# Where the first stage's weight loads are issued, and where the last stage waits for cleared buffers, in a four-layer kernel on one core

## What is computed

```python
x = L0_attn_x                                             # (2, 2048, 256)
x = x + ln(window_attention(ln(x), w_attn, w_proj))       # 16 heads, windows of 64
x = x + ln(moe(ln(x)))                                    # 8 experts, top 2, and a shared SwiGLU
x = x + ln(gated_linear_attention(ln(x)))                 # causal, 16 heads, gate, affine norm
x = x + ln(gated_recurrence(ln(x)))                       # scan over the leading axis, tanh head
```

```python
qkv = x @ w_attn.T;  q, k, v = split(qkv)                 # heads of 16
att = softmax(q @ k.T / sqrt(16))                         # within each window of 64 tokens
y = (att @ v) @ w_proj.T
```

## Time and profile before

| | us |
|---|---|
| median of three runs | 1522.32 |
| lowest and highest | 1518.44, 1523.31 |
| the profiled execution, its own time | 1526.08 |
| its span, first to last instruction | 1524.2 |
| PE busy in the span | 1431.7 |

### The profile page before, as it was taken

The page is one execution under the profiler, slowest core; times in us unless marked ns, Lnnn a source line. Parts: engine busy times, 40 slices in busy tenths (PEclk is TensorE's granted clock), DMA queues, the critical chain, the costliest instruction groups (busy, mean ns, idle before and its releaser), DMA issues. The chain is left out here.

```text
span 1524.2 us, 36248 instructions
## 1 busy us (share of the span) xinstructions
PE 1431.7 (94%) x13257; PEld 1248.6 (82%) x13257; DVE 871.3 (57%) x1979; ACT 712.5 (47%) x1656; POOL 603.5 (40%) x1133
## 2 busy tenths in 40 slices
PE   5999999898999999999999997998999999999985
PEld 4888888687899999999999997876777777777865
DVE  3888888364333334333433331366788888888762
ACT  3666666221344444454445442334555555555542
POOL 2565555213122222212221112434657775775432
PEclk9999999899899999999999998999999999999988
DMA  5333433253011111111111112521111211121000
GB/s 197 96 120 106 123 107 100 64 158 118 28 36 49 43 43 42 44 46 42 39 42 50 42 43 73 163 70 43 40 60 44 64 56 52 43 64 33 9 15 21
DMA packets 88044, 100.10 MB, mean 66 GB/s; under 512 B 12384, under 2 KB 74720, under 8 KB 87872
## 3 DMA queue, kind: packets, MB, share of 16 engines
q1 hardware_dynamic: 77824, 75.53, 15.9%
q0 software_dynamic: 6480, 17.70, 4.1%
q10 hardware_dynamic: 3568, 4.55, 0.9%
HBM read 63.28 MB, written 34.47 MB: 64 GB/s over the span
## 5 line engine op out<-in xcount | busy, mean ns | idle before, releaser
L895 PEld LDWEIGHTS ex_hb<-ex_xT,lane_w 128*128 128x128 f32 x3124 | 362.6, 193 | 6.5 <-issue 2.8
L895 PE MATMUL ex_hb<-ex_xT,lane_w 128*128 128x128 f32 x3124 | 363.2, 276 | 2.4 <-ACT lane_w L891 2.4
L998 DVE TENSOR_TENSOR ex_gT<-ex_gT,ex_hb 128x384 f32<-128x384 f32 (+1 forms) x142 | 69.2, 488 | 334.8 <-ACT ex_gT L961 306.9
L869 POOL COPY slot_idx<-source 128x1 int32<-128x1 int32 x69 | 37.4, 543 | 413.3 <-PE ex_xb L922 413.3
L931 PE MATMUL ex_yb<-w,ex_gT 128*128 x852 | 195.7, 379 | 1.6 <-DVE ex_gT L1000 1.6
L959 ACT ACTIVATE ex_gT<-ex_hb 128x384 f32<-128x384 f32 (+1 forms) x142 | 62.0, 437 | 247.2 <-PE ex_hb L895 246.6
L931 PEld LDWEIGHTS ex_yb<-w,ex_gT 128*128 128x128 f32 x852 | 156.3, 190 | 20.1 <-issue 1.8
L891 ACT COPY lane_w<-w 128x1408 f32 x71 | 96.9, 1365 | 7.9 <-issue 1.7
L1072 POOL TENSOR_SCALAR la_ln_ve<-la_ln_mv 128x1 f32<-128x1 f32 x128 | 33.6, 262 | 155.0 <-DVE la_ln_mv L1065 150.0
L1643 POOL DMA_INDIRECT la_a<-yg,place x64 | 69.0, 1079 | 49.9 <-POOLq L55 34.7
L1402 DVE TENSOR_TENSOR la_em<-la_E,consts 128x512 f32<-128x512 f32 x128 | 79.3, 682 | 6.9 <-PE la_E L1356 6.5
(11 more groups left out here) (263 smaller groups left out, 3162.8 us busy)
## 6 DMA issues: line engine op xcount, KB each, us to landing
yg<-ex_yo SPq DMA_DIRECT2D x71, 128.0 KB
w<-in_w SPq DMA_DIRECT2D x16, 384.0 KB, 4.9
w<-in_w SPq DMA_DIRECT2D x16, 352.0 KB
w<-in_w SPq DMA_DIRECT2D x16, 320.0 KB
wa_xa<-in_x SPq DMA_DIRECT2D x32, 128.0 KB
x<-wa_xo SPq DMA_DIRECT2D x32, 128.0 KB
xn<-wa_xn SPq DMA_DIRECT2D x32, 128.0 KB, 3.6
xn1T<-wa_x1T SPq DMA_DIRECT2D x32, 128.0 KB, 3.6
```

Source lines behind the costliest of these rows:

```text
L869: e.tensor_copy(d["idx"][:], source[:, i:i + 1]).then_inc(S["idx"], 1)
L895: o = e.matmul(out, lane_w[:, i % 2, k, at:at + P], B[i % 2]["xT"][:, k, :], start=(k == 0), stop=(k == KC - 1))
L998: o = e.tensor_tensor(g, g, chunks(hb[2 * half + 1][:, 0:n], c1 - c0), ALU.mult)
```

## The change

Five things, none of which alters a number that is computed:

- The constants come in two loads. `first` is now columns 0 to 132 (`ident`, `half`, `head_of_16`; 68 KB), and `others` the remaining 887. DVE waits for `others` before the routing's choice, PE before its prefix sums.
- `wqkv` comes in three column ranges. `keys` is the middle one (256 KB), with a semaphore of its own, and `own` is the other two and `wp`. PE waits for `keys` ahead of its first key matmul and for `own` ahead of its first query matmul. ACT issues `first`, `keys`, `own`, `others`: six DMAs.
- DVE clears `vb` at once, and sets the ones at `s == 2`, behind the first tile's statistics. ACT waits for `vb_set` ahead of its first two writes to `vb`.
- `shared` and `later` are issued by SP, behind x of tile 3 and of tile 5. The pieces of `w13` go out behind x of tiles 2, 4, ... 30 and 31, so none at tile 0.
- In `attention_recurrence` the three waits for `zero` stand at the first use: ACT in step 4, PE and DVE in step 5.

```diff
-        first = Loads(nc, "l_consts", [(consts[:], A["consts"])])
+        n = sum(lay[k].shape[1] for k in ("ident", "half", "head_of_16"))
+        first = Loads(nc, "l_consts", [(consts[:, 0:n], A["consts"][:, 0:n])])
+        others = Loads(nc, "l_more", [(consts[:, n:], A["consts"][:, n:])])
...
-        own = Loads(nc, "l_wa", [(wqkv[:], kcn(A["w_attnT"])), (wp[:], kcn(A["w_projT"]))])
+        keys = Loads(nc, "l_wk", [(wqkv[:, :, C:2 * C], kcn(A["w_attnT"])[:, :, C:2 * C])])
+        own = Loads(nc, "l_wa", [(wqkv[:, :, 0:C], kcn(A["w_attnT"])[:, :, 0:C]),
+                                 (wqkv[:, :, 2 * C:3 * C], kcn(A["w_attnT"])[:, :, 2 * C:3 * C]), (wp[:], kcn(A["w_projT"]))])
...
-                    if i % 2 == 0:
-                        for dst, src in w13_piece(i // 2):
+                    if i >= 2 and i % 2 == 0 or i == NT - 1:
+                        for dst, src in w13_piece((i - 1) // 2):
                             e.dma_start(dst, src).then_inc(S["w13"], 16)
+                    if i == 3:
+                        shared.start(e)
+                    if i == 5:
+                        later.start(e)
...
         def tensor(e):
             first.wait(e)
-            own.wait(e)
...
                     e.wait_ge(S["xnT"], i + 1)
+                    if i == 0:
+                        keys.wait(e)
...
                         e.wait_ge(S["vb"], i)
+                    else:
+                        own.wait(e)
...
-            first.wait(e)
             e.memset(B[0]["vb"][:], 0.0).then_inc(S["set"], 1)
-            e.wait_ge(S["set"], 2)
-            for d in B:
-                for w in range(2):
-                    for h2 in range(2):
-                        o = e.memset(d["vb"][64 * h2:64 * h2 + 64, w, :, h2, D:D + 1], 1.0)
-            o.then_inc(S["vb_set"], 1)
             for s in range(STEPS):
+                if s == 2:
+                    first.wait(e)
+                    e.wait_ge(S["set"], 2)
...
+                    o.then_inc(S["vb_set"], 1)
...
             first.start(e)
+            keys.start(e)
             own.start(e)
-            e.wait_ge(S["vb_set"], 1)
+            others.start(e)
             for s in range(STEPS):
-                if s == 2:
-                    shared.start(e)
-                if s == 4:
-                    later.start(e)
...
                         e.wait_ge(S["pv"], i - 1)
+                    else:
+                        e.wait_ge(S["vb_set"], 1)
```

21 lines of the change are left out of this document (15 added, 6 removed).

## The result

| | before | changed |
|---|---|---|
| median (us) | 1522.12, 6 runs | 1512.18, 6 runs |
| lowest and highest | 1517.76, 1525.55 | 1508.80, 1516.29 |
| ratio, 95% interval | | 0.9938, 0.9919 to 0.9956 |
| the profiled execution, its own time | 1526.08 | 1516.29 |

The changed kernel is 9.9 us faster by the medians, and 0.62% by the ratio. Timed a second time on another occasion it took 1510.29 us (1504.37 to 1515.05, 6 runs), beside 1523.48 for the kernel before (11 runs): 13.2 us, ratio 0.9919, 0.9896 to 0.9943. Most of the distance between single runs goes with the mean granted clock: 1504.37 at 0.989, about 1510 at 0.985, 1515 to 1516 at 0.980.

What follows compares the result with a forecast made beforehand. Two chains of short steps, at the start and in the last stage, were taken to bound it; 3.6 + 3.9 + 2.6 = 10.1 us off 1526.08 gave 1516.0, as a median 1512.2, with 8 in 10 between 1507.5 and 1518.

Steps and rivals of the forecast that it cites:

- A: First tile: split loads, later ones in vb and w13 pieces; norm at 6.0, gain 3.6 us (2.5 to 4.4).
- B: Third tile: shared and later issued by SyncE; no idle time or low clock, gain 3.9 us (2.4 to 4.4).
- C: Last stage's start: moved waits for zero let TensorE's late tiles begin earlier, gain 2.6 us (1.4 to 2.9).
- the landing of x: Kernel start: first x and small constants land at 3.8 us, between 3.0 at the earliest and 4.9 at the latest.
- The table load: ScalarE at the start: six issues end at 3.7 us and the table load at 5.0, before the shift is complete.
- The weights: First tile: keys through at 4.0 us and own at 6.0, with 3.9 and 3.8 us to spare.
- near 26.6: Sign of being right, first stage: the third scores come near 26.6 us instead of 34.16.
- SyncE's queue at no cost: First stage: twelve more issues on SyncE cost 0, and up to 0.5 us at the stage's end.
- The third rival, starvation: First stage: SyncE's longer queue makes x land late, most likely tile 4's, and the kernel slower; chance 0.03.
- does the gain last?: Last stage, step 3: the wait for the later la_fx moves along with TensorE's chain, so the gain of 2.6 us stays.
- The first rival: Start and last stage: late landings of x and la_fx replace the removed waits; 1514.5 to 1516.0 us, chance 0.13.
- rival 2: Between 271 and 400 us: more time at the lower clock costs 5 us; about 1517 to 1520 us, chance 0.12.

Runs made afterwards that it cites:

- e3: A alone: the changed kernel with shared and later back on ScalarE and the waits for zero back ahead of the loops; one run, 1520.90 us.
- the repeat: The changed kernel as it is, timed and traced once more on another occasion; 1510.29 us (6 runs), ratio 0.9919.
- B alone: The kernel before, with only the twelve loads of shared and later moved from ScalarE to SyncE; one run, 1518.39 us.
- e5: The changed kernel with nine idle matmuls of zeros at the start of TensorE's stream; 1513.48 us (8 runs), ratio 0.9936.
- e14: The changed kernel with the waits for zero back ahead of the loops and GpSimd's two clears moved ahead of its gathers; one run, 1505.23 us.
- e4: The changed kernel with the three waits for zero back ahead of the loops (A and B without C); one run, 1516.00 us.
- e11: The same kernel as e4 (the changed kernel with the three waits back ahead of the loops), timed; 1513.37 us (9 runs), ratio 0.9947.

## Why the prediction was right

The time came out where the sum had it (1512.2), and most steps hold: both causes at the start and the one in the last stage are what the traces show. That it came out to a tenth is luck. The kernel's own median was 1512.18 and 1510.29 on two occasions, single runs spread over 12 us, and several sizes inside the sum were off and cancelled. The stretches on the average give 7.6 us for A and B and 2.8 for C, 10.4 together where the sum has 10.1.

- **A, first load and first norm: right, and a little small.** The working had statistics at 3.8 and the norm at 6.0, for a gain of 3.6 with an upper bound of 4.4. Measured are 3.23 and 5.34, a gain of 4.29. The term that was off is the landing of x: the sum has it at 3.7, which is 3.0 us from issue to landing, and it took 2.5. Its reason for going half a microsecond below the store, the write that a load lacks, is shown by no run. The table load was over before the shift, as reckoned, but only because both edits are there: the four issues that B takes away from ahead of it hold the norm at 7.11 (e3). The working didn't say that neither edit brings all of this alone. The weights landed at 4.6 (`keys`) and 6.8 (the last of `own`), later than the 4.0 and 6.0 reckoned, and still in time for the matmuls at 7.21 and 9.07.
- **A, whether the gain lasts: wrong in the profiled run.** The step took the first tile's slow matmuls to end with the first tile, as in the trace of before. In the profiled execution they lasted 0.7 us longer in the first tile, and the clock fell again in the second (1.6 us), so that of 4.28 us 2.00 was left at the second scores. The repeat shows 4.69 there (22.94 - 18.25). The third scores, a sign of being right at "near 26.6", came at 28.09, and at 25.37 in the repeat. The rivals named a fall at another place, between 271 and 400 us, not this one.
- **B, eight loads off ScalarE: right.** Gain 3.9 in the sum, 11.22 - 7.15 = 4.07 in the changed kernel, 4.10 in B alone, and 0.24 in A alone. Both halves show in A alone: 2.93 us of idle time, and keys at 2.08 instead of 1.16 us.
- **A and B together** were 7.5 us in the sum. The end of part I moved by 6.1 us in the profiled run, by 8.7 in the repeat, and by 7.6 in the mean of the seven traces with A, B and no idle matmuls (256.90 against 264.50). Alone they moved it by 0.35 and 3.3: less than together, as the first norm needs both.
- **SyncE's queue at no cost: right.** No load of x appears among VectorE's waits behind the first tile, and the steps of 7.35 and later 8.01 us are those of before. The third rival, starvation, is out.
- **C: right in the sum, wrong in the way.** The working had `la_fx` landing at 3.6 us or later after its issue, so that the late work would begin 2.6 us earlier. It began 3.09 earlier, at once behind the small matmuls, as the load was there by then. How soon it lands shows in e5 and e14, where the small matmuls are over sooner and that load is TensorE's releaser: 2.2 and 2.4 us after the issue. Taking the time of a store for it was the mistake. The step "does the gain last?" looked at the wait for the later `la_fx` and held it to be harmless. What it missed is the stall up to 12.2 us: of the 3.09, 1.45 us was left at GpSimd's first `la_x`. Later it was 2.3 us at the query-key matmuls, with the wait for `la_fx` down from 2.05 to 1.13, and 2.4 at VectorE's last product, so the size agrees with the 2.6 of the sum, in part by luck. The first rival, another wait in place of the removed one, is in part true of this place, though the wait isn't the landing that it names.
- **The clock, rival 2.** Parts II and IV vary by several microseconds, but for kernels with the same instructions as well, and before and changed profiles have nearly the same in part II (676.88 and 676.71, both with 0.89 in the stretch of the earlier trace rows). So the profiled comparison was spared, and the medians show no sign of it. One kernel's part II differs by up to 5.2 us between executions (e4 and e11); that an earlier start makes it worse, as the rival says, no run shows.
- **Against the profiled run's own time** the sum gave 1516.0, and the profiled execution took 1516.29: 6.1 us from part I, 0.2 from II, 2.4 from III and 1.1 from IV make up the 9.8. Here too luck has a share: part I gave 1.4 us less than the 7.5 of the sum, and part IV, which no edit touches, gave 1.1.

## What to carry to other kernels

Read the first microseconds of a kernel as a chain of landings: what the first tile's chain needs goes out first and alone, since a large load beside it delays the small one too, even for an engine that doesn't wait for the large one. DMA issues of later weights don't belong in the stream of an engine whose next instruction releases TensorE; a gap of 2.4 us on TensorE there cost another 1.7 at the lower clock (keys, queries and values of one tile, before the change). Where two edits clear the same wait, test them together and apart. With single runs that spread over 12 us, a gain of 2 or 3 us shows in stretches of several traces and not in medians of six.

## What the hardware showed that I had not expected

- The same instructions had the lower clock in the second tile in some executions and not in others (second scores at 18.25 and at 20.94). It was at the lower level with the DMA engines idle (share 0.02, e3) and at the higher with them full (1.03, the changed kernel's repeat).
- Nine matmuls of zeros on otherwise idle TensorE (18 records, 0.98 to 5.19 us) took the keys of the first tile from 2.07 to 1.16 us and shortened part I by 1.6 us or more, which eight timed runs (1513.48 us) don't show.
- In nine traces in which TensorE took up the late tiles by 3.1 us after the last stage's start, its results stopped until 12.1 to 12.3 us after it, while its recorded matmuls end 2.3 us before (in the changed kernel's trace). Two traces without the early start have a trace of the same instant (12.12 and 12.20). No trace shows the cause.
- The first x (128 KB) landed 2.5 us after its issue beside a first load of 66.5 KB, and 1.2 to 1.6 us later beside one of 502 KB from another queue.
